# Attention block: the output projection as three products of rounded parts, with the parts made on GpSimd

## The chip, the cores and the metric

The kernel is one program on one core of a Trainium2 chip. The metric is the device time of one execution in microseconds (us). A core has five engines with queues of their own: TensorE (PE, matrix products; PEld is its loading of weights), VectorE (DVE), ScalarE (ACT), GpSimd (POOL) and SyncE (SP), which here issues the transfers. They meet only at semaphores: an instruction adds to one when it is done, and another engine's queue waits until it has reached a number.

## The reference, cut to what matters

The program computes, on an input of 8 x 512 x 256: a delta-rule attention, a feed-forward block, the attention block of this case, and the same feed-forward block again, each with a layer norm before and the input added behind. The attention block has 16 query heads in 4 groups, each group with one key and one value head of 128:

```python
x = x + attn_b(layernorm(x), Wq, Wk, Wv, Wg, Wd, Wo)

# inside attn_b; b = 8, s = 512, 4 groups n of 4 heads g, head size 128
scores = einsum('bngqd,bnkd->bngqk', q, k) * scale
logits = where(causal & (bias > 0), scores + bias, neg)
p = softmax(logits, axis=-1)
o = einsum('bngqk,bnkd->bngqd', p, v)
o = o.transpose(0, 3, 1, 2, 4).reshape(b, s, 16 * 128)
return o @ Wo                      # Wo: 2048 x 256
```

Everything is float32. The change is in the last line.

## The kernel before

The program is a row of five stages, each with its own buffers and semaphores: tables, delta rule, first feed-forward (names `f_`), attention (names `a_`), second feed-forward (names `h_`). Between two stages all engines meet.

In the attention stage the work is cut into 32 turns. Turn t is batch b and group n (t = 4b + n); `here` and `there` are the buffers of even and odd turns. All turns but those of the first and last batch lie in a hardware loop that covers two batches. Each engine's order within a turn is written out by hand in its `turn` function, and everything that an engine waits for is a semaphore count. A turn handles four heads g, shifted against each other so that the engines overlap. For head g:

- TensorE computes the query (`query`, three products of rounded parts), then the scores of four row tiles (`scores`), tiles 0 and 1 before the next query and tiles 2 and 3 behind it. Two PSUM banks `sc` take turns, so tile i + 2 needs tile i read.
- VectorE reads each score tile in `logits` (L2146: score tile in PSUM and bias in SBUF to `pr`, and a row minimum `low`); ScalarE takes the exponentials; VectorE scales the rows in `normalise` (three small chained instructions, L2172 to L2174, and four scalings, L2176, of 128 to 512 columns).
- TensorE transposes the probabilities (`turn_probs`) and multiplies them with the values (`values`, into the one bank `out`); VectorE adds the tail rows and stores the result (`head_out`, L2166) to `oT`, 128 channels x 512 rows, in a slot for each head. `values` of the next head waits for that.

The output projection of turn t - 1 stands in turn t, in two halves of two row tiles each (`project_out`, L1828): the first behind `values` of head 0, the second behind `values` of head 1. A half is 8 full-precision products of 128x128 by 128x256, summed over the four heads; the trace records two matmuls for each. Its end is counted in `y`. VectorE adds a half to the residual `x` (`add_out`, L2186). In the turn, behind the second `add_out`, VectorE makes the low part of the next-but-one turn's query and key weights (`split_w`, L2120). In turns with n = 2 and 3 TensorE computes value rows of the next batch behind the second half; in turn n = 2 it also computes the gate rows.

A "rounded part" is float32r, a shortened float32 that TensorE takes in fewer passes: x_hi is x written as float32r, x_lo is x - x_hi written as float32r, and `product` sums hi x hi, lo x hi and hi x lo.

GpSimd has little to do in this stage: in each turn a diagonal matrix of flags (`diagonals`, L2306) and three copies of bias rows (`spread`, L2298). The projection's weights come by a transfer for each turn (`load_wo`) into two buffers `wo`, and `oT` has two buffers as well, so a projection of turn t - 1 and the heads of turn t don't meet.

Of the kernel before, what the change touches and what calls it, by code (L numbers as in the profile page):

```python
# [10 lines left out]
ALU = mybir.AluOpType  # L11
# [4 lines left out]
P = 128  # L16
# [1567 lines left out]
def attention(nc, io, sems, src, dst):  # L1584
# [6 lines left out]
    with ExitStack() as ctx:  # L1591
# [8 lines left out]

        s = {n: sems[f"a_{n}"] for n in ATTN_SEMS}
        const = sb("const", [P, NCONST])
        cc = {k: const[:, lo:hi] for k, (lo, hi) in CONSTS.items()}
        ident = cc["ident"]
# [10 lines left out]
        wv_hi, wv_lo = (sb(f"wv_{i}", [P, KD, NK * P], F32R) for i in ("hi", "lo"))  # L1615
        wo = two("wo", [P, G, D])
        xl, x, xn = sb("xl", [P, TT, D]), two("x", [P, TT, D]), sb("xn", [P, TT, D])
# [14 lines left out]
        pt = two("pt", [P, L * TT - P * 6])  # L1632
        oT = two("oT", [P, G, L])

# [25 lines left out]
        def _(sp):  # L1660
# [10 lines left out]

            def load_wo(n, tp_):
                sp.dma_start(wo[tp_][:], io["wo_b"][n * G * P:(n + 1) * G * P].rearrange("(g p) d -> p g d", p=P)).then_inc(s[f"wo{tp_}"], 16)

# [11 lines left out]
            load_norm(0)  # L1686
            sp.dma_start(const[:], io["consts"]).then_inc(s["in"], 16)
            load_w(0)
# [15 lines left out]
            def turn(b, bp, n, t, begin, more):  # L1704
                if more or n < 2:
                    sp.wait_ge(s["w_lo"], t + 2)
                    load_w((n + 2) % HKV)
                if not (isinstance(t, int) and t < 2):
                    sp.wait_ge(s["y"], 2 * t - 2)
                load_wo(n, n % 2)  # L1710
                head = isinstance(b, int) and b == 0
                if n == 0 and more:
                    sp.wait_ge(s["xn"], b + 1)
                    load_norm(b + 1)
                if n == 1:
                    if not head:
                        store(b - 1, 1 - bp)
                if n == 2 and more:
                    if not head:
                        sp.wait_ge(s[f"out{1 - bp}"], 8 * b + 8 * bp)  # L1720
                        load_x(b + 1, 1 - bp)
                    sp.wait_ge(s["keep"], b + 2)
                    if not head:
                        sp.wait_ge(s["bp"], HKV * b)
                        sp.wait_ge(s["bd"], HKV * b)
                    else:
                        sp.wait_ge(s["wv_lo"], 1)
                    spread(b + 1, 1 - bp)
# [8 lines left out]
        def _(pe):  # L1737
# [85 lines left out]
            def project_out(t, tp_, half):  # L1823
                if half == 0:
                    pe.wait_ge(s["oT"], G * t + G)
                for j, m in enumerate((2 * half, 2 * half + 1)):
                    for g in range(G):
                        mm = M.matmul(pb[:, j * D:(j + 1) * D], oT[tp_][:, g, m * P:(m + 1) * P], wo[tp_][:, g, :], start=(g == 0), stop=(g == G - 1))  # L1828
                mm.then_inc(s["y"], 1)

            def wo_count(t, n):

                return 8 * t + (0 if n % 2 == 0 else 8)

            def turn(b, bp, n, t, begin, more):
# [52 lines left out]
                if not begin:  # L1888
                    pe.wait_ge(s[f"wo{there}"], wo_count(t, n))
# [69 lines left out]
            values(LAST, HKV - 1, 3, 1)  # L1959
            pe.wait_ge(s["wo1"], 8 * B * HKV)  # L1960
            pe.wait_ge(s["xadd"], 2 * LAST)
# [106 lines left out]
        def _(dve):  # L2068
# [93 lines left out]
            def head_out(t, tp_, g):  # L2162

                dve.wait_ge(s["pv"], G * t + g + 1)
                dve.wait_ge(s["frow"], t + 1)
                V.tensor_tensor(oT[tp_][:, g, :], out[:], tl[tp_][:], ALU.add).then_inc(s["oT"], 1)  # L2166

# [117 lines left out]
        def _(pool):  # L2285
# [15 lines left out]
            def diagonals(t):  # L2301

                pool.wait_ge(s["fl"], t + 1)
                if not (isinstance(t, int) and t == 0):
                    pool.wait_ge(s["ftr"], t)
                Gp.tensor_tensor(dg[:], cc["ident"].unsqueeze(1).to_broadcast([P, TAIL, P]), fl[:].unsqueeze(2).to_broadcast([P, TAIL, P]),  # L2306
                                 ALU.mult).then_inc(s["dg"], 1)

            def turn(b, bp, n, t, begin, more):
# [12 lines left out]
            loop(pool, turn)  # L2322


ATTN_SEMS = ["xl", "x0", "x1", "in", "w", "wv", "wo0", "wo1", "out0", "out1", "kept", "kb0", "kb1",
             "gd", "gd_hi", "gd_lo", "tr", "x_hi", "x_lo", "gt", "gc", "sig", "keep", "vp", "v", "vtp", "vtT", "dg", "one", "w_hi", "w_lo", "wv_hi", "wv_lo",
# [81 lines left out]
```

## Time and profile before

| | before |
| --- | --- |
| median of 3 runs | 4455.96 us (4451.16 to 4456.58) |
| profiled execution, its own time | 4464.27 us |
| its span, first to last instruction | 4462.2 us |
| TensorE busy over the span | 4129.1 us (93%) |
| VectorE | 3010.4 us (67%) |
| ScalarE | 2183.5 us (49%) |
| GpSimd | 1201.0 us (27%) |
| mean granted TensorE clock | 0.973 |

The attention stage lies between about 2898 us and 4241 us of the span. A row of the timeline gives start, duration, engine, line of the kernel, operation, output <- inputs, shape and count; in brackets stands how long the engine was idle before it and which instruction ended that. A row of the groups gives the total, the mean in ns, and the idle time before. Matmuls overlap: the distance of two starts tells what one costs, not its duration. The two levels of TensorE's clock are 2.4 GHz (granted clock 1.0) and 1.2 GHz (0.5).

### The profile page before, as it was taken

The numbers are of one execution on the slowest core, as the hardware profiler recorded it, in microseconds if no ns is written. First come the engines' busy times: TensorE is split into PE (matmuls) and PEld (weight loads), VectorE is DVE, ScalarE is ACT, GpSimd is POOL, SyncE is SP. The second block draws the span as 40 slices with busy tenths as digits, with TensorE's granted clock in tenths as the row PEclk, the third lists the DMA queues.
The fourth block names the chain that finished last, engine by engine and source line by source line (L and its number), as shares of the span: only waits on it lengthen the run. The fifth ranks groups of instructions, "written<-read, shape, count | busy, mean of one in ns | idle before, by whom it ended". The sixth has DMA issues, their size and how long they took to land. (4 is left out here: it accounts for less than half of the span.)

```text
span 4462.2 us, 97071 instructions
## 1 busy us (share of the span) xinstructions
PE 4129.1 (93%) x32143; PEld 3442.7 (77%) x32143; DVE 3010.4 (67%) x7897; ACT 2183.5 (49%) x5660; POOL 1201.0 (27%) x2727
## 2 busy tenths in 40 slices
PE   3499999999999999999999779879999999999979
PEld 3388888888888888888888668767777777778768
DVE  5577777777777777777777345346776776776655
ACT  2255555555555555555555234334444444444344
POOL 5244444444444444444444100000000000000000
PEclk9999999999999999999999689979999999999989
DMA  6433433333333343333333132131111111111021
GB/s 253 150 100 101 120 114 106 106 102 109 100 110 99 107 123 106 104 110 100 109 100 101 59 134 85 41 98 41 38 51 52 52 32 52 52 47 42 15 68 34
DMA packets 558447, 393.06 MB, mean 88 GB/s; under 512 B 253040, under 2 KB 504944, under 8 KB 556400
## 3 DMA queue, kind: packets, MB, share of 16 engines
q1 hardware_dynamic: 557936, 386.69, 28.1%
q8 instruction: 267, 4.37, 0.4%
q14 instruction: 244, 2.00, 0.2%
HBM read 288.36 MB, written 98.14 MB: 87 GB/s over the span
## 5 line engine op out<-in xcount | busy, mean ns | idle before, releaser
L962 DVE SCALAR_TENSOR_TENSOR g_conv<-g_r,g_taps,g_conv 128x511 f32<-128x511 f32 (+2 forms) x961 | 700.0, 742 | 135.9 <-ACT g_conv L847 127.6
L851 ACT ACTIVATE g_us<-g_chn 128x128 f32<-128x128 f32 x528 | 146.6, 278 | 688.4 <-PE g_chn L646 687.6
L2001 ACT ACTIVATE a_pr<-a_pr,a_low 128x128 f32<-128x128 f32 (+3 forms) x512 | 286.6, 560 | 396.2 <-DVE a_low L2146 380.3
L1152 POOL TENSOR_TENSOR g_prod<-g_small 64x14 f32<-64x14 f32 (+6 forms) x896 | 227.0, 253 | 665.8 <-DMA g_small<-lower_d 600.2
L571 PE MATMUL g_r<-g_x_hi,g_w_hi 128*128 128x512 f32 x770 | 366.9, 477 | 9.6 <-issue 7.1
L2146 DVE CUSTOM_DVE_ANT_0 a_pr<-a_sc,a_bias 128x128 f32<-128x128 f32 (+3 forms) x512 | 242.2, 486 | 193.2 <-issue 174.2
L2306 POOL TENSOR_TENSOR a_dg<-a_const,a_fl 128x384 fp32r<-128x384 f32 x32 | 26.4, 826 | 1154.5 <-DVE a_fl L2153 1154.5
L571 PE MATMUL g_r<-g_x_hi,g_w_lo 128*128 128x512 f32 x770 | 306.8, 398 | 0.0
L571 PE MATMUL g_r<-g_x_lo,g_w_hi 128*128 128x512 f32 x770 | 305.0, 396 | 0.0
L1820 PE MATMUL a_out<-a_pt,a_v 128*128 128x512 f32 (+3 forms) x1024 | 297.9, 434 | 0.9 <-DVE a_oT L2166 0.9
L847 ACT ACTIVATE g_conv<-g_r,g_taps 128x512 f32<-128x512 f32 x321 | 220.4, 687 | 137.4 <-PE g_r L571 127.0
L1820 PEld LDWEIGHTS a_out<-a_pt,a_v 128*128 128x128 f32 x1024 | 185.0, 191 | 103.1 <-issue 62.6
L995 DVE SCALAR_TENSOR_TENSOR g_R<-g_chn,g_ctab,g_bv 128x128 f32<-128x128 f32 x462 | 160.4, 347 | 150.9 <-PE g_chn L638 136.7
L1154 POOL TENSOR_TENSOR g_small<-g_small,g_prod 64x14 f32<-64x14 f32 (+6 forms) x896 | 240.6, 269 | 70.3
L1828 PE MATMUL a_pb<-a_wo,a_oT 128*128 128x256 f32 x1024 | 231.8, 379 | 1.7 <-DVE a_oT L2166 0.9
L1003 DVE SCALAR_TENSOR_TENSOR g_S<-g_S,g_ctab,g_chn 128x128 f32<-128x128 f32 x396 | 137.2, 346 | 134.7 <-PE g_chn L656 134.7
L646 PE MATMUL g_chn<-g_R,g_U 128*128 128x128 f32 x924 | 213.9, 314 | 8.3 <-DVE g_R L995 6.9
L638 PE MATMUL g_chn<-g_S,g_kT 128*128 128x128 f32 x924 | 205.1, 304 | 13.8 <-DVE g_S L1001 10.9
L658 PE MATMUL g_ob<-g_us,g_at 128*128 128x128 f32 x1056 | 214.6, 286 | 0.4 <-ACT g_us L851 0.4
L987 DVE TENSOR_TENSOR g_U<-g_U,g_lev 64x128 f32<-64x128 f32 x520 | 147.8, 284 | 93.7 <-PE g_lev L611 88.2
L1828 PEld LDWEIGHTS a_pb<-a_wo,a_oT 128*128 128x128 f32 x1024 | 189.7, 190 | 25.3 <-DVE a_x L2186 1.2
L1745 PE MATMUL a_sc<-a_k_hi,a_q_hi 128*128 128x128 f32 (+3 forms) x512 | 185.4, 362 | 25.6 <-DVE a_low L2146 19.0
(355 smaller groups left out, 11714.6 us busy)
## 6 DMA issues: line engine op xcount, KB each, us to landing
g_w_hi<-ws_d SPq DMA_DIRECT2D x65, 768.0 KB, 5.5
g_w_lo<-ws_d SPq DMA_DIRECT2D x65, 768.0 KB, 6.7
lower_d<-g_L SPq DMA_DIRECT2D x64, 512.0 KB, 3.3
g_T<-low_d SPq DMA_DIRECT2D x64, 512.0 KB, 4.1
g_U<-upp_d SPq DMA_DIRECT2D x64, 512.0 KB, 5.4
a_w<-w_groups SPq DMA_DIRECT2D x32, 640.0 KB, 4.5
oT_d<-g_oT SPq DMA_DIRECT2D x67, 256.0 KB, 5.4
f_oT<-oT_d SPq DMA_DIRECT2D x8, 2048.0 KB, 9.4
```

The source lines that it names most:

```text
L571: mm = M.matmul(BANK[n][:], a[:, k, n, :], c[:, k, :], start=(i == 0), stop=(i == len(terms) - 1))
L638: M.matmul(chn[:, 0, :], keys[:, c, :], S[c % 2][:], start=True, stop=True).then_inc(s["d_ks"], 1)
L646: M.matmul(chn[:, 1, :], U[par][:, c, :], bv[par][:, 0, :] if c == 0 else R[:], start=True, stop=True).then_inc(s["d_u"], 1)
L658: mm = M.matmul(dst, at[(q + 2) % QN][:, c, :], us[:], start=(c % 2 == 0), stop=False)
L847: A(conv[TURN[n] % 2][:], BANK[n][:], ACT.Copy, scale=taps[par][:, n, CONV - 1:CONV]).then_inc(s["d_tap"], 1)
L962: ins = V.scalar_tensor_tensor(out=y[:, k:L], in0=x[:, 0:L - k], scalar=tap, in1=y[:, k:L], op0=ALU.mult, op1=ALU.add)
L1152: ch.link(G.tensor_tensor(prod[:, 0:SM - 1 - k, 0:k], small[:, k + 1:SM, k:k + 1].to_broadcast(shape), small[:, k:k + 1, 0:k].to_broadcast ...
L1154: ch.link(G.tensor_tensor(rest, rest, prod[:, 0:SM - 1 - k, 0:k], ALU.subtract))
L1820: mm = M.matmul(out[:, k * P:L], v[bp][:, k, at], pt[g % 2][:, first[k]:first[k] + L - k * P], start=(k == 0), stop=(k == TT - 1))
L1828: mm = M.matmul(pb[:, j * D:(j + 1) * D], oT[tp_][:, g, m * P:(m + 1) * P], wo[tp_][:, g, :], start=(g == 0), stop=(g == G - 1))
L2001: A(pr[g % 2][:, i, 0:width(i)], pr[g % 2][:, i, 0:width(i)], ACT.Exp, scale=-1.0, bias=low[g % 2][:, i:i + 1], accum_out=tot[g % 2][:, i: ...
L2146: V.tensor_tensor_reduce(pr[g % 2][:, i, 0:width(i)], sc[i % 2][:, 0:width(i)], bias[tp_][:, i, 0:width(i)], -SCALE, 3.0e38, ALU.add, ALU. ...
```

## The change

The projection becomes a `product` of rounded parts: three products in place of one full-precision product, 24 matmuls in a half. GpSimd makes the parts: `split_head` those of a head's output (a multiplication with ones that writes float32r, then a subtraction, 128x512 each), `split_wo` those of the turn's weights (128x1024 each). `oT` is now two buffers of one head each; the parts `o_hi`, `o_lo`, `wo_hi`, `wo_lo` and the loaded weights `wo` exist once. So `split_wo(t)` and the heads 0 to 2 of turn t wait for `y` at 2t, the end of the projection of turn t - 1; `head_out` waits until its buffer's former head has been split; `project_out` waits for the parts, and the load of the weights for the split of those before. GpSimd's order in a turn is: diagonals, head 3 of the turn before, bias rows, weights, heads 0, 1 and 2. The stage loads only the 1808 columns of the constants that it uses, out of 2320.

```diff
-        const = sb("const", [P, NCONST])
+        USED = CONSTS["pick_group"][1]
+        const = sb("const", [P, USED])
-        wo = two("wo", [P, G, D])
+        wo = sb("wo", [P, G, D])
+        wo_hi, wo_lo = (sb(f"wo_{i}", [P, G, D], F32R) for i in ("hi", "lo"))
-        oT = two("oT", [P, G, L])
+        oT = two("oT", [P, L])
+        o_hi, o_lo = (sb(f"o_{i}", [P, G, L], F32R) for i in ("hi", "lo"))
...
-                if not (isinstance(t, int) and t < 2):
-                    sp.wait_ge(s["y"], 2 * t - 2)
-                load_wo(n, n % 2)
+                if not begin:
+                    sp.wait_ge(s["wo_lo"], t)
+                load_wo(n)
...
             def project_out(t, tp_, half):
                 if half == 0:
-                    pe.wait_ge(s["oT"], G * t + G)
+                    pe.wait_ge(s["o_lo"], G * t + G)
+                    pe.wait_ge(s["wo_lo"], t + 1)
                 for j, m in enumerate((2 * half, 2 * half + 1)):
-                    for g in range(G):
-                        mm = M.matmul(pb[:, j * D:(j + 1) * D], oT[tp_][:, g, m * P:(m + 1) * P], wo[tp_][:, g, :], start=(g == 0), stop=(g == G - 1))
+                    at = slice(m * P, (m + 1) * P)
+                    mm = product(pb[:, j * D:(j + 1) * D], [(o_hi[:, g, at], o_lo[:, g, at], wo_hi[:, g, :], wo_lo[:, g, :]) for g in range(G)])
                 mm.then_inc(s["y"], 1)
...
                 dve.wait_ge(s["frow"], t + 1)
-                V.tensor_tensor(oT[tp_][:, g, :], out[:], tl[tp_][:], ALU.add).then_inc(s["oT"], 1)
+                if not (isinstance(t, int) and G * t + g < 2):
+                    dve.wait_ge(s["o_lo"], G * t + g - 1)
+                V.tensor_tensor(oT[g % 2][:], out[:], tl[tp_][:], ALU.add).then_inc(s["oT"], 1)
...
+            def split_head(t, g):
+                pool.wait_ge(s["oT"], G * t + g + 1)
+                Gp.tensor_tensor(blocks(o_hi[:, g, :]), blocks(oT[g % 2][:]), by_one(TT), ALU.mult).then_inc(s["o_hi"], 1)
+                pool.wait_ge(s["o_hi"], G * t + g + 1)
+                Gp.tensor_tensor(o_lo[:, g, :], oT[g % 2][:], o_hi[:, g, :], ALU.subtract).then_inc(s["o_lo"], 1)
+
+            def split_wo(t):
+                flat = lambda m: m[:].rearrange("p g d -> p (g d)")
+                pool.wait_ge(s["wo"], 16 * t + 16)
+                Gp.tensor_tensor(blocks(flat(wo_hi)), blocks(flat(wo)), by_one(G * D // P), ALU.mult).then_inc(s["wo_hi"], 1)
+                pool.wait_ge(s["wo_hi"], t + 1)
+                Gp.tensor_tensor(flat(wo_lo), flat(wo), flat(wo_hi), ALU.subtract).then_inc(s["wo_lo"], 1)
+
             def turn(b, bp, n, t, begin, more):
...
                 diagonals(t)
+                if not begin:
+                    split_head(t - 1, G - 1)
                 if nxt:
...
                     spread(1 - n % 2, (n + 1) % HKV, nb, 8 * b - 8 * bp + 16 if n < HKV - 1 else 8 * b + 8 * bp + 16)
+                if not begin:
+                    pool.wait_ge(s["y"], 2 * t)
+                split_wo(t)
+                for g in range(G - 1):
+                    split_head(t, g)
...
             loop(pool, turn)
+            split_head(LAST, G - 1)
```

## Rows read from the trace of the kernel before

**Rows 1.** Stretch: length, busy (x instructions) of PE, PEld, DVE, ACT, POOL; clock; DMA.
```profile
3100.00:4240.00 1140.00, 1105.56 (x5764) 895.16 (x5762) 795.93 (x2842) 525.17 (x1365) 69.31 (x109) 0.99 0.14 43
```

**Rows 2.** Timeline of TensorE, a turn with n = 1.
```profile
3515.14 3.62 PE L1828 MATMUL a_pb<-a_wo,a_oT 128*128 128x256 f32 x16
...
3518.66 0.28 PE L1745 MATMUL a_sc<-a_k_hi,a_q_lo 128*128 128x128 f32 x1
...
3518.88 0.33 PE L1745 MATMUL a_sc<-a_k_hi,a_q_hi 128*128 128x256 f32 x1
3519.05 0.28 PE L1745 MATMUL a_sc<-a_k_hi,a_q_lo 128*128 128x256 f32 x1
...
3521.16 0.44 PE L1745 MATMUL a_sc<-a_k_hi,a_q_hi 128*128 128x384 f32 x1 [0.31 <-DVE a_low L2146]
...
3528.75 0.45 PE L1745 MATMUL a_sc<-a_k_hi,a_q_hi 128*128 128x384 f32 x1 [0.32 <-DVE a_low L2146]
```

**Rows 3.** Timeline of TensorE in the first feed-forward stage, first and last of 46.
```profile
2886.07 0.28 PE L1318 MATMUL f_wide<-f_w_lo,f_h_hi 128*128 128x256 f32 x1
...
2891.17 0.28 PE L1318 MATMUL f_wide<-f_w_lo,f_h_hi 128*128 128x256 f32 x1
```

**Rows 4.** GpSimd's groups; the last row: ns least/median/most, first and last start.
```profile
L1165 POOL TENSOR_TENSOR g_dmt<-g_dmt,g_const 128x512 f32<-128x512 f32 x64 | 82.2, 1284 | 3.2 <-ACT g_dmt L866 2.2 <-issue 1.0
...
L1568 POOL TENSOR_TENSOR f_xb<-f_x,f_b 128x1024 f32<-128x1024 f32 x8 | 19.2, 2400 | 265.6 <-DVE f_mark L1482 265.6
...
L2306 POOL TENSOR_TENSOR a_dg<-a_const,a_fl x32: 825/826/828, 2968.2 to 4197.3; 128x384 fp32r<-128x384 f32 x32
```

**Rows 5.** Timeline of VectorE in the turn of rows 2.
```profile
3518.80 0.69 DVE L2186 TENSOR_TENSOR a_x<-a_x,a_pb 128x512 f32<-128x512 f32 x1 [2.42 <-PE a_pb L1828]
3519.40 1.48 DVE L2120 TENSOR_TENSOR a_w_lo<-a_w,a_w_hi 128x1280 fp32r<-128x1280 f32 x1
...
3524.91 0.53 DVE L2173 TENSOR_TENSOR a_cnt<-a_cnt,a_tot 128x4 f32<-128x4 f32 x1
...
3525.69 1.59 DVE L2176 TENSOR_SCALAR a_pr<-a_pr,a_rec 128x128 f32<-128x128 f32 x4
3527.20 0.68 DVE L2166 TENSOR_TENSOR a_oT<-a_out,a_tl 128x512 f32<-128x512 f32 x1
...
3576.99 0.16 DVE L2173 TENSOR_TENSOR a_cnt<-a_cnt,a_tot 128x4 f32<-128x4 f32 x1
...
3577.40 1.27 DVE L2176 TENSOR_SCALAR a_pr<-a_pr,a_rec 128x128 f32<-128x128 f32 x4
```

**Rows 6.** Timeline of GpSimd in that turn: the bias rows.
```profile
3524.45 1.75 POOL L2298 TENSOR_TENSOR a_bias<-a_kb,a_start 128x128 f32<-128x128 f32 x3
```

**Rows 7.** Timeline of the first stage: the first of four GpSimd splits, VectorE's scalings.
```profile
12.89 3.42 POOL L230 TENSOR_TENSOR t_wh_hi<-t_wh,t_const 128x1536 fp32r<-128x1536 f32 x1 [9.65 <-DMA t_wh<-w_heads]
...
13.90 12.96 DVE L320 TENSOR_SCALAR t_xn<-t_x,t_mv,t_rstd 128x256 f32<-128x256 f32 x4
```

**Rows 8.** Timeline of VectorE and TensorE, a turn with n = 2 and the start of the next.
```profile
3561.28 0.69 DVE L2186 TENSOR_TENSOR a_x<-a_x,a_pb 128x512 f32<-128x512 f32 x1 [2.41 <-PE a_pb L1828]
...
3565.61 0.33 PE L1745 MATMUL a_sc<-a_k_hi,a_q_hi 128*128 128x384 f32 x1
...
3573.56 0.33 PE L1745 MATMUL a_sc<-a_k_hi,a_q_hi 128*128 128x384 f32 x1
```

**Rows 9.** Timeline of TensorE, a turn with n = 0: the query behind the key.
```profile
3623.17 0.50 PE L1745 MATMUL a_pa<-a_x_hi,a_w_hi 128*128 128x512 f32 x1 [0.73 <-DVE a_k_lo L2134]
```

**Rows 10.** Timeline of TensorE at the end of the stage: the last projections.
```profile
4221.81 3.62 PE L1828 MATMUL a_pb<-a_wo,a_oT 128*128 128x256 f32 x16
...
4232.83 3.69 PE L1828 MATMUL a_pb<-a_wo,a_oT 128*128 128x256 f32 x16 [0.88 <-DVE a_oT L2166]
```

**Rows 11.** Timeline of TensorE, one long idle; granted clock (third last number) behind it.
```profile
3447.13 0.32 PE L1745 MATMUL a_sc<-a_k_hi,a_q_hi 128*128 128x128 f32 x1 [3.21 <-issue]
...
3448.00:3463.00 15.00, 14.66 (x71) 11.74 (x70) 7.77 (x31) 4.95 (x14) 0.00 (x0) 0.77 0.01 2
```

More of the change, by code:

```diff
@@ L1601, in attention @@
         s = {n: sems[f"a_{n}"] for n in ATTN_SEMS}
-        const = sb("const", [P, NCONST])
-        cc = {k: const[:, lo:hi] for k, (lo, hi) in CONSTS.items()}
+        USED = CONSTS["pick_group"][1]
+        const = sb("const", [P, USED])
+        cc = {k: const[:, lo:hi] for k, (lo, hi) in CONSTS.items() if hi <= USED}
         ident = cc["ident"]
@@ L1670, in load_w, with load_wo @@
                 sp.dma_start(w[:], io["w_groups"][n, :, :, 0:GW]).then_inc(s["w"], 16)
-            def load_wo(n, tp_):
-                sp.dma_start(wo[tp_][:], io["wo_b"][n * G * P:(n + 1) * G * P].rearrange("(g p) d -> p g d", p=P)).then_inc(s[f"wo{tp_}"], 16)
+            def load_wo(n):
+                sp.dma_start(wo[:], io["wo_b"][n * G * P:(n + 1) * G * P].rearrange("(g p) d -> p g d", p=P)).then_inc(s["wo"], 16)
             def spread(b, bp):
@@ L1686, in _ @@
             load_norm(0)
-            sp.dma_start(const[:], io["consts"]).then_inc(s["in"], 16)
+            sp.dma_start(const[:], io["consts"][:, 0:USED]).then_inc(s["in"], 16)
             load_w(0)
@@ L1824, in project_out @@
                 if half == 0:
-                    pe.wait_ge(s["oT"], G * t + G)
+                    pe.wait_ge(s["o_lo"], G * t + G)
+                    pe.wait_ge(s["wo_lo"], t + 1)
                 for j, m in enumerate((2 * half, 2 * half + 1)):
-                    for g in range(G):
-                        mm = M.matmul(pb[:, j * D:(j + 1) * D], oT[tp_][:, g, m * P:(m + 1) * P], wo[tp_][:, g, :], start=(g == 0), stop=(g == G - 1))
+                    at = slice(m * P, (m + 1) * P)
+                    mm = product(pb[:, j * D:(j + 1) * D], [(o_hi[:, g, at], o_lo[:, g, at], wo_hi[:, g, :], wo_lo[:, g, :]) for g in range(G)])
                 mm.then_inc(s["y"], 1)
-            def wo_count(t, n):
-                return 8 * t + (0 if n % 2 == 0 else 8)
             def turn(b, bp, n, t, begin, more):
@@ L1888, in turn @@
                 if not begin:
-                    pe.wait_ge(s[f"wo{there}"], wo_count(t, n))
                     if n == 0 or not more:
@@ L1959, in _ @@
             values(LAST, HKV - 1, 3, 1)
-            pe.wait_ge(s["wo1"], 8 * B * HKV)
             pe.wait_ge(s["xadd"], 2 * LAST)
@@ L2307, in diagonals @@
                                  ALU.mult).then_inc(s["dg"], 1)
+            by_one = lambda n: cc["ones"].unsqueeze(1).to_broadcast([P, n, P])
+            blocks = lambda ap: ap.rearrange("p (n c) -> p n c", c=P)
+            def split_head(t, g):
[9 more added lines that the diff above has]
+                Gp.tensor_tensor(flat(wo_lo), flat(wo), flat(wo_hi), ALU.subtract).then_inc(s["wo_lo"], 1)
             def turn(b, bp, n, t, begin, more):
@@ L2322, in _ @@
             loop(pool, turn)
-ATTN_SEMS = ["xl", "x0", "x1", "in", "w", "wv", "wo0", "wo1", "out0", "out1", "kept", "kb0", "kb1",
+            split_head(LAST, G - 1)
+ATTN_SEMS = ["xl", "x0", "x1", "in", "w", "wv", "wo", "wo_hi", "wo_lo", "o_hi", "o_lo", "out0", "out1", "kept", "kb0", "kb1",
              "gd", "gd_hi", "gd_lo", "tr", "x_hi", "x_lo", "gt", "gc", "sig", "keep", "vp", "v", "vtp", "vtT", "dg", "one", "w_hi", "w_lo", "wv_hi", "wv_lo",
```

## The prediction

> **What bounds the kernel now.** I read the page first, then the stretches of the attention stage, then one turn on TensorE, VectorE and GpSimd side by side. The change lies in the attention stage alone. It runs from about 2898 us to 4241 us. In its steady part TensorE is busy 97% of the time at a granted clock of 0.99, VectorE 70% and GpSimd 6% [rows 1]. So TensorE sets the time, and GpSimd looks like a free engine. What the shares hide is how tightly VectorE follows TensorE. In the turn around 3515 us TensorE already idles twice, 0.31 and 0.32 us, each time before the third score tile of a head, until `logits` has read the bank (L2146) [rows 2]. Whatever delays VectorE ahead of those two places is lost by TensorE one for one.
>
> **The products.** A half of the projection is 16 recorded matmuls (two for each of 8 full-precision products). The first starts at 3515.14; the next work's second matmul starts at 3518.66, and such matmuls are 0.11 apart (3518.66 to 3518.88 holds two intervals) [rows 2], so the half takes 3.52 - 0.11 = 3.4 us. The new half is 24 matmuls on rounded parts, 256 columns wide. The feed-forward stage has just that stream: from 2886.07 to 2891.17 us there are 45 starts of this shape, 0.113 us apart [rows 3]. 24 x 0.113 = 2.7 us. Saved: 0.68 us per half, 64 halves, 43.5 us. The lower bound comes from the score product of 256 columns behind one of 128, whose first interval is 0.17 (18.88 to 19.05) [rows 2]; if each of the 8 groups paid it, a half would take 8 x 0.40 = 3.2 us and the saving would be 13 us. I take 43.5, the row of the same shape.
>
> **What GpSimd gets.** The tensor operations in its list with two streamed operands give the price: 1.28 us for 128x512, 2.40 us for 128x1024 [rows 4]. A head is two of 128x512 (2.54 us), the weights are two of 128x1024 (4.7 us): 4 x 2.54 + 4.7 = 14.9 us in a turn of 39.6 us (31 turns between the first and the last start of the diagonals, L2306) [rows 4], beside 0.83 + 1.75 = 2.6 us now [rows 4, 6]. The capacity is there. The place is the trouble. The weights of a turn are split only after y(2t), the end of the second projection half, because `wo_hi` and `o_hi` are single; head 0 is split behind them. So right after each second half GpSimd works 4.7 + 2.5 + 2.5 us without a pause, head 1 included.
>
> **The wait of head_out.** VectorE's `head_out(t,2)` now waits for head 0's parts, 7.3 us after y. Before, it starts 8.4 us after the add that follows y (3518.80 to 3527.20) [rows 5]. By itself this wait is just hidden.
>
> **VectorE beside GpSimd.** This is the large term. At 3524.91 a 128x4 addition of two SBUF operands (L2173) takes 0.53 us where its other calls take 0.16, and the four scalings after it take 1.59 us where 1.27 is usual [rows 5]; in exactly that time GpSimd is copying bias rows [rows 6]. The first stage shows it large: four scalings of 128x256 take 12.96 us while GpSimd runs its 3.42 us splits one behind the other [rows 7]. That is one VectorE instruction per GpSimd instruction. VectorE's work on PSUM with one SBUF operand (L2146, L2166) keeps its length. The Trainium skill, page "SBUF — State Buffer", section "SBUF: two separate sides", calls this an exclusive lock on a port pair shared by the two engines, taken by a DVE instruction in a 2-port mode or with two SBUF inputs, and held for the whole instruction. It speaks against this change, and the trace agrees; with full GpSimd durations as the blocks its rule would make the loss of a turn some 0.5 us larger than what I take next.
>
> I walk through a turn with the times after the add of half two (zero at 3518.80, [rows 5]).
> - Turns with n = 0 or 1 (no value rows behind the half). GpSimd's first weight split covers 0.05 to 2.4. `split_w` (L2120, two SBUF operands, 1.48 us) wants 0.60 and gets in at about 2.2: `logits` is 1.6 late, and TensorE, which already waits there, loses 1.6. Then the second weight split and head 0 hold GpSimd until 7.5 to 8.7, head 1 until 10.2 to 11.4. In this time fall the count instruction (L2172), the addition (L2173) and the four scalings of `normalise`. They are chained, so each of the three gets in behind another GpSimd instruction, the four scalings together behind one: end at 11.3 to 12.5 instead of 8.5. `head_out` and the next `logits` are 2.8 to 4.0 late in all, and TensorE with them. I take 3.5 us. There are 15 such turns: 52 us (42 to 62).
> - Turns with n = 2 or 3 (value rows first). Zero is 3561.28 [rows 8]. `split_w` is late by 1.6 again and ends at 3.7; `logits` behind it has read the first tile at 4.1. TensorE, with the value rows before it, wants the third tile at 3565.61, which is 4.33 [rows 8]: nothing lost. `normalise` then ends 1.5 to 2.1 late. The next `logits` stands behind it, with 1.1 us of slack before TensorE wants its third score tile at 3573.56 [rows 8]; 0.4 to 1.0 is lost. I take 0.8, 14 turns: 11 us (0 to 18).
> - The diagonal of the mask (L2126, two SBUF operands) meets the split of head 3, up to 0.85 us. Behind it VectorE makes the key's low part, for which TensorE already waits 0.73 us in a turn with n = 0 [rows 9]; there and in the others the wait for ScalarE's part or the gate and value rows cover most of it. 0.15 us x 30: 5 us (0 to 15).
>
> **The end of the stage.** The last turn has no further scores behind half two, which starts at 4221.81 and ends 3.4 us later, at 4225.2. Before, the last projection starts at 4232.83 [rows 10]. Now it comes after 4.7 + 4 x 2.54 us of GpSimd work, with its hops 15.6 us after 4225.2, at 4240.8: +8 us. Nothing hides this. The bound below is 7, above 11 with the slow clock.
>
> **The clock.** After TensorE's idle of 3.21 us at 3447.13 the granted clock falls to a mean of 0.77 over the next 15 us, that is 7 us of the stretch at the lower level (1.2 instead of 2.4 GHz) [rows 11]. The new idle comes in two pieces, each under 2 us. I add 5 us (0 to 40).
>
> **Small ones.** The constants shrink from 2320 to 1808 columns, once, ahead of the stage's first matmul; no row prices it, a gain under 1 us, left out of the sum. The weights' load waits for the split of the turn before (about 6 us after y) and has 25 us left. On GpSimd `diagonals` moves behind head 2 and `spread` behind head 3. Head 2 can only be split once `head_out(t,2)` has run, so behind a turn with n = 1 the diagonals are ready at about 16.6 us after the zero, while TensorE does the scores, the transposes and the values of head 3 that stand ahead of their matmul (L1797): hidden, but by little. This cover is the next to go: with GpSimd later still, TensorE waits for the diagonals. `spread` is needed only at the end of the turn. Extra semaphore clears: nothing, under 0.5 us.
>
> **Sum.** 52 + 11 + 5 + 8 + 5 - 43.5 = +37.5 us. The profiled execution took 4464.27 us, its span 4462.2, the median of the three runs 4455.96; I carry the same difference over: 4456 + 37.5 = 4493 us. The likeliest case has a range of its own of 4460 to 4530: the low bounds give 42 + 7 - 44 = +5, the high ones, with 10 us of clock and a saving of 35, 62 + 18 + 15 + 11 + 10 - 35 = +81, which takes all blocks at once.
>
> **Rivals.**
> 1. The products decide and the blocks are mostly absorbed. For it: VectorE is idle 30% of the stage. Against: [rows 5, 7]. Then -43.5 + 7 = -37, 4419 us; with a fifth of the 68 us of blocks left, 4432. It decides in favour as soon as the blocked turns cost under 1.2 us on the mean. Chance 0.16.
> 2. The blocks are worse. GpSimd could get in between the four unchained scalings of `normalise` as well, as it did between the chained ones of [rows 7]; another two blocks of 1.0 us in 29 turns is +58, and with the clock falling in the 15 turns with two idle pieces (3.4 us each, [rows 11]) +50. That gives 4550 to 4600. Chance 0.14.
> 3. Gain and loss cancel within 9 us: the low bounds of my own case. Chance 0.08.
> 4. My case: 0.62.
>
> 0.2% (9 us) is about what a measurement of this kernel can tell from no change. Faster: rival 1, 0.16. Same: 0.08. Slower: 0.76. The range for 8 in 10 goes from 4432 to 4560.
>
> **What the changed profile would show.** The projection's 24 matmuls per half should start 0.113 us apart. TensorE's share in the steady part should fall from 97% to about 90%, with its idle put down to `a_low` L2146 and to what follows `split_w`. `split_w` should last about 3 us instead of 1.48, L2173 and L2176 should have means well over 0.25 and 0.40 us. GpSimd's new instructions should last 1.27 and 2.35 us. Before the last projection TensorE should idle about 8 us more. I am wrong if `split_w` keeps 1.48 us beside a running GpSimd split (then rival 1), if the three-part products start more than 0.13 us apart, or if GpSimd's instructions are themselves stretched by VectorE, so that the wait for `o_lo` in `head_out` becomes the one that ends last.

## The result and the profile after

The changed kernel (called after from here on, as the old one is called before) takes 4529.18 us (median of 4 runs, 4523.01 to 4533.61) against 4456.27 us (4451.16 to 4459.46): ratio 1.0156, 95% interval 1.0143 to 1.0169, 72.9 us slower. The forecast was 4493, in a range of 4432 to 4560: the direction was right, the loss twice as large as forecast (37.5). The profiled execution took 4533.61 us. First the page of after, span and busy shares:

```profile
span 4531.8 us, 98557 instructions
...
PE 4120.6 (91%) x32655; PEld 3455.3 (76%) x32655; DVE 3140.7 (69%) x7897; ACT 2180.1 (48%) x5660; POOL 1722.9 (38%) x3047
```

The stretches of after (columns as in [rows 1]): the steady part, which answers to [rows 1], and the whole attention stage.

```profile
3100.00:4300.00 1200.00, 1098.97 (x6248) 905.46 (x6246) 920.37 (x2867) 526.72 (x1379) 545.20 (x404) 0.96 0.14 41
...
2931.00:4313.00 1382.00, 1249.05 (x7014) 1029.77 (x7013) 1035.04 (x3222) 596.01 (x1550) 601.58 (x448) 0.95 0.14 41
```

The same whole stage before:

```profile
2935.00:4242.00 1307.00, 1255.51 (x6497) 1015.62 (x6497) 902.89 (x3222) 599.71 (x1550) 81.72 (x128) 0.98 0.14 44
```

All of the loss is here: 75 us, with 4 us less ahead of the stage. TensorE's share in the steady part is 92%. Over the whole stage its idle rises from 51.5 to 133 us, and its busy time, which the cheaper products should have cut by over 40 us, falls by 6 at a lower granted clock (0.95 instead of 0.98). That looks like two losses of their own, 80 us of waits and 40 us of clock. The last two experiments show that much of the second is hidden in the first.

GpSimd's and VectorE's groups of after:

```profile
L2317 POOL TENSOR_TENSOR a_o_lo<-a_oT,a_o_hi 128x512 fp32r<-128x512 f32 x128 | 171.6, 1341 | 10.0
...
L2325 POOL TENSOR_TENSOR a_wo_lo<-a_wo,a_wo_hi 128x1024 fp32r<-128x1024 f32 x32 | 109.3, 3414 | 2.5
...
L2118 DVE TENSOR_TENSOR a_w_lo<-a_w,a_w_hi 128x1280 fp32r<-128x1280 f32 x30 | 95.4, 3179 | 0.0
...
L2173 DVE TENSOR_TENSOR a_cnt<-a_cnt,a_tot 128x4 f32<-128x4 f32 x128 | 50.2, 392 | 4.4
...
L2151 DVE TENSOR_SCALAR a_fl<-a_low 128x3 f32<-128x3 f32 x32 | 26.9, 839 | 1.1
```

`split_w` (L2118 now) takes 3.18 us instead of 1.48 on average over these 30 calls; 29 of them take 3.16 us or more. Who waits for whom on TensorE (us in total, times, longest), in after from 2980 to 4300 us:

```profile
PE a_sc L1748 <- DVE a_low L2144: 80.6, 46, 5.0
PE a_pa L1748 <- DVE a_k_lo L2132: 10.0, 13, 1.4
PE a_out L1823 <- DVE a_oT L2166: 5.1, 1, 5.1
```

and before, from 2980 to 4230 us:

```profile
PE a_sc L1745 <- DVE a_low L2146: 13.6, 38, 3.0
```

Up to the last turn TensorE does not wait for a part made by GpSimd. It waits for `logits` on VectorE, 67 us more than before. One turn with n = 0 (the half's add, L2186, to the first `logits` of the next head) on VectorE, after:

```profile
3167.02 0.69 DVE L2186 TENSOR_TENSOR a_x<-a_x,a_pb 128x512 f32<-128x512 f32 x1 [0.20 <-PE a_pb L1748]
3167.62 3.25 DVE L2118 TENSOR_TENSOR a_w_lo<-a_w,a_w_hi 128x1280 fp32r<-128x1280 f32 x1
...
3173.74 0.62 DVE L2151 TENSOR_SCALAR a_fl<-a_low 128x3 f32<-128x3 f32 x1
...
3175.74 1.19 DVE L2173 TENSOR_TENSOR a_cnt<-a_cnt,a_tot 128x4 f32<-128x4 f32 x1
...
3177.18 2.16 DVE L2176 TENSOR_SCALAR a_pr<-a_pr,a_rec 128x128 f32<-128x128 f32 x4
...
3179.87 0.28 DVE L2144 CUSTOM_DVE_ANT_0 a_pr<-a_sc,a_bias 128x128 f32<-128x128 f32 x1
```

and on GpSimd in the same time:

```profile
3167.15 2.38 POOL L2323 TENSOR_TENSOR a_wo_hi<-a_wo,a_const 128x1024 fp32r<-128x1024 f32 x1 [18.05 <-PE a_pb L1748]
3169.61 3.50 POOL L2325 TENSOR_TENSOR a_wo_lo<-a_wo,a_wo_hi 128x1024 fp32r<-128x1024 f32 x1
3173.07 1.26 POOL L2315 TENSOR_TENSOR a_o_hi<-a_oT,a_const 128x512 fp32r<-128x512 f32 x1
...
3175.64 1.28 POOL L2315 TENSOR_TENSOR a_o_hi<-a_oT,a_const 128x512 fp32r<-128x512 f32 x1
3176.99 1.28 POOL L2317 TENSOR_TENSOR a_o_lo<-a_oT,a_o_hi 128x512 fp32r<-128x512 f32 x1
```

`split_w` ends 1.34 us after GpSimd's first weight split (3169.53), so it did nearly all of its 1.48 us of work behind it. The addition L2173 ends at 3176.93, where the split begun at 3175.64 ends (3176.92). From the add to the next `logits` VectorE needs 12.85 us. TensorE pays at two places, each ahead of the third score tile of a head (first and second place from here on); here the turn with n = 0 and the next:

```profile
3171.15 0.44 PE L1748 MATMUL a_sc<-a_k_hi,a_q_hi 128*128 128x384 f32 x1 [2.08 <-DVE a_low L2144]
3180.21 0.44 PE L1748 MATMUL a_sc<-a_k_hi,a_q_hi 128*128 128x384 f32 x1 [0.60 <-DVE a_low L2144]
...
3210.93 0.44 PE L1748 MATMUL a_sc<-a_k_hi,a_q_hi 128*128 128x384 f32 x1 [2.08 <-DVE a_low L2144]
3220.63 0.45 PE L1748 MATMUL a_sc<-a_k_hi,a_q_hi 128*128 128x384 f32 x1 [2.44 <-DVE a_low L2144]
```

The end of the stage on TensorE: last matmul of half two, then the start of the last projection. Between them lie the two idles that GpSimd's parts do cause: 5.1 us before the values of head 3, since the `head_out` of head 2 waits 6.2 us for `a_o_lo`, and 3.51 us before the projection, until GpSimd's last subtraction ends at 4302.85.

```profile
4286.93 0.28 PE L1748 MATMUL a_pb<-a_wo_lo,a_o_hi 128*128 128x256 f32 x1
...
4302.95 0.55 PE L1748 MATMUL a_pb<-a_wo_hi,a_o_hi 128*128 128x256 f32 x1 [3.51 <-issue]
```

### The profile page after: what moved, and what is told of

It is laid out like the page before. It is cut to its first block and busy times, and to the rows that moved or that the text cites. A ratio compares the mean times of both kernels' runs of the same rounds, so it can differ in the third digit from the quotient of the medians.

```text
span 4531.8 us, 98557 instructions
## 1 busy us (share of the span) xinstructions
PE 4120.6 (91%) x32655; PEld 3455.3 (76%) x32655; DVE 3140.7 (69%) x7897; ACT 2180.1 (48%) x5660; POOL 1722.9 (38%) x3047
## 5 line engine op out<-in xcount | busy, mean ns | idle before, releaser
L2323 POOL TENSOR_TENSOR a_wo_hi<-a_wo,a_const 128x1024 fp32r<-128x1024 f32 x32 | 76.2, 2382 | 541.6 <-PE a_pb L1748 541.6
L1143 POOL TENSOR_TENSOR g_gsum<-g_tab,g_const 128x512 fp32r<-128x512 f32 x65 | 68.0, 1047 | 513.5 <-DMA g_tab<-tab_d 513.4
L2315 POOL TENSOR_TENSOR a_o_hi<-a_oT,a_const 128x512 fp32r<-128x512 f32 x128 | 163.5, 1277 | 185.4 <-DVE a_oT L2166 185.4
```

## The experiments

The times of different runs are compared as they stand. The kernel before was measured again beside them, and its median was 4456 to 4462 us, so a difference of two such times is good to some 6 us.

**What does GpSimd's work cost?** The parts are made of 4 columns only; the rest of each is filled with ones once. The other three operations are cut in the same way. Nearly all of the projection's values are left out. All waits and all of TensorE's work stay.

```diff
-                Gp.tensor_tensor(blocks(o_hi[:, g, :]), blocks(oT[g % 2][:]), by_one(TT), ALU.mult).then_inc(s["o_hi"], 1)
+                Gp.tensor_tensor(o_hi[:, g, 0:4], oT[g % 2][:, 0:4], cc["ones"][:, 0:4], ALU.mult).then_inc(s["o_hi"], 1)
...
```

> The changed kernel with all its waits, buffers and orders, but GpSimd makes the parts of 4 columns only (both splits of a head and both of the weights), each about 0.2 us; the rest of the parts is filled once with ones, so most of the projection's values are left out. If the loss comes from VectorE being held behind GpSimd's long instructions, it is gone and the gain of the products is left: 4456 - 43 = 4413 us, 4405 to 4425, and split_w lasts 1.48 us. If it comes from the new waits (single buffers, the weights only after y), most of it stays: above 4480.

Measured: 4417.18 us, ratio 0.9899 (0.9881 to 0.9917). `split_w` is at 1.49 us again, L2173 at 0.175. So the waits and the order cost nothing that shows; the length of GpSimd's instructions costs 112 us (4529.2 - 4417.2), with what the clock does in consequence. The same turn on VectorE in this kernel:

```profile
3153.41 0.69 DVE L2186 TENSOR_TENSOR a_x<-a_x,a_pb 128x512 f32<-128x512 f32 x1 [0.20 <-PE a_pb L1748]
3154.01 1.49 DVE L2118 TENSOR_TENSOR a_w_lo<-a_w,a_w_hi 128x1280 fp32r<-128x1280 f32 x1
...
3159.53 0.16 DVE L2173 TENSOR_TENSOR a_cnt<-a_cnt,a_tot 128x4 f32<-128x4 f32 x1
...
3159.94 1.28 DVE L2176 TENSOR_SCALAR a_pr<-a_pr,a_rec 128x128 f32<-128x128 f32 x4
...
3161.73 0.29 DVE L2144 CUSTOM_DVE_ANT_0 a_pr<-a_sc,a_bias 128x128 f32<-128x128 f32 x1
```

8.32 us to the next `logits`, against 12.85.

**What do the products give?** All of GpSimd's work stays, and the projection is done as before, in full precision, on the high parts; the low parts are made and not used.

```diff
-                    mm = product(pb[:, j * D:(j + 1) * D], [(o_hi[:, g, at], o_lo[:, g, at], wo_hi[:, g, :], wo_lo[:, g, :]) for g in range(G)])
+                    for g in range(G):
+                        mm = M.matmul(pb[:, j * D:(j + 1) * D], o_hi[:, g, at].bitcast(F32), wo_hi[:, g, :].bitcast(F32), start=(g == 0), stop=(g == G - 1))
```

> The changed kernel with GpSimd's work and all waits, but the projection is again one full-precision product, of the high parts alone (the low parts are made and not used). If TensorE's saving of 0.68 us per half comes through in full in the changed kernel, this takes 43 us more than it: 4572 us. If TensorE gives part of it back by waiting for VectorE, less: 4540 to 4560. Were the saving an error of mine, 4529.

Measured: 4577.61 us, ratio 1.0254 (1.0237 to 1.0271). The products give back 48.4 us (4577.6 - 4529.2); the prediction had 43.5. Beside this run the kernel before took 5.6 us more than beside the change, and by the two ratios (1.0254 and 1.0156) it is 44 us. In the traces a turn with n = 2 at full clock is 1.45 us longer than in after, 46 us in 32 turns. So the saving lies between 44 and 48 us.

**Is it what GpSimd reads, or that it runs?** Each split becomes a 4-column operation and a fill of a buffer that nobody reads (no input, 0.95 us each, one for each part of a head, two for each part of the weights). The values are left out as in the first run.

```diff
+                Gp.tensor_tensor(o_hi[:, g, 0:4], oT[g % 2][:, 0:4], cc["ones"][:, 0:4], ALU.mult)
+                Gp.memset(fill[:, 0, :], 1.0).then_inc(s["o_hi"], 1)
...
```

> The changed kernel with GpSimd's splits replaced by one operation on 4 columns and fills of a scratch buffer, meant to last about as long as the splits (a fill reads nothing from SBUF); parts filled once with ones, so the projection's values are left out. If only GpSimd's reads hold VectorE up: like small parts plus the late end, 4413 + 8 = 4421 us. If any long GpSimd instruction does: about 4520. If it holds up the one-operand scalings and the flags but not the instructions with two SBUF operands, between: 4450 to 4490, with split_w at 1.48 us and L2176 and L2151 long.

Measured: 4442.92 us, ratio 0.9951 (0.9935 to 0.9968). The groups on VectorE, lines shifted by one:

```profile
L2119 DVE TENSOR_TENSOR a_w_lo<-a_w,a_w_hi 128x1280 fp32r<-128x1280 f32 x30 | 44.5, 1484 | 0.0
...
L2152 DVE TENSOR_SCALAR a_fl<-a_low 128x3 f32<-128x3 f32 x32 | 25.9, 811 | 1.1
...
L2174 DVE TENSOR_TENSOR a_cnt<-a_cnt,a_tot 128x4 f32<-128x4 f32 x128 | 22.4, 175 | 4.4
...
3165.61 2.63 DVE L2177 TENSOR_SCALAR a_pr<-a_pr,a_rec 128x128 f32<-128x128 f32 x4
```

Beside a GpSimd that only writes, VectorE's instructions with two SBUF operands run free (1.48 and 0.175 us), while the short one with a single SBUF operand is still at 0.81 instead of 0.17 (0.73 without its first call, which stands beside the one-time filling of the parts). The four scalings, also of one SBUF operand, take 2.63 us instead of 1.27 in the turns with n = 0 and 1 (the last row is one of them). The Trainium skill, page "SBUF — State Buffer", section "Who interferes with whom", states this division: a VectorE instruction with two SBUF inputs is blocked only by a GpSimd instruction that reads SBUF, one in a 2-port mode by any. The trace agrees for the instructions with two SBUF inputs; in which mode the others run, it does not show. GpSimd is busy 108 us less here than in after (1614.7 against 1722.9), so the 86 us between the two runs (4529.2 - 4442.9) are not all due to the reads.

**Would another order help?** GpSimd's split of the weights waits for VectorE's `split_w`.

```diff
                 if not begin:
                     pool.wait_ge(s["y"], 2 * t)
+                    if more or n < 2:
+                        pool.wait_ge(s["w_lo"], t + 3)
                 split_wo(t)
```

> The changed kernel, complete, with one wait more: GpSimd starts the weights' split only when VectorE's split_w of the turn is done. split_w goes from a mean of 3.18 us back to 1.48, which by my walk gives back 1.6 us in each of the 15 turns with n = 0 or 1; GpSimd is 1.4 us later, so flags and normalise meet more of it. By the theory of the blocks a gain of 0 to 25 us: 4505 to 4529. If late parts (the wait of head_out) were what matters: 20 to 40 us slower.

Measured: 4576.45 us, ratio 1.025 (1.0233 to 1.0267): a clear miss, 47 us slower than after instead of somewhat faster. `split_w` is free indeed (1484 ns), but GpSimd's 10 us of work now begin 2 us later and lie over all of `normalise`. VectorE in a turn with n = 2, the addition and the four scalings:

```profile
3616.79 1.29 DVE L2173 TENSOR_TENSOR a_cnt<-a_cnt,a_tot 128x4 f32<-128x4 f32 x1
...
3618.33 3.09 DVE L2176 TENSOR_SCALAR a_pr<-a_pr,a_rec 128x128 f32<-128x128 f32 x4
```

The scalings take 3.09 us instead of 1.27: a GpSimd instruction gets in between them, though they aren't chained (4.26 us in turns with n = 0 and 1). That is the mechanism of rival 2; in after the four take 2.0 to 2.2 us in all turns but the last two. Yet `head_out`, which stands behind them, starts only 0.5 to 0.7 us later than in after, some 17 us in 30 turns. The rest of the 47 goes with the clock: behind the halves of the turns with n = 1 TensorE's two idle places are of 0.3 and 4.7 us instead of 2.08 and mostly 2.4, and the granted clock up to the next second half is 0.89 instead of mostly 0.96. No run separates the two parts. My picture, that the block of `split_w` can be saved by itself, fell: a block avoided comes back at the next VectorE instruction of the kind, as long as GpSimd's list is as long.

**Weights or heads?** Weights split in full, heads of 4 columns (the heads' values are left out):

```diff
...
-                Gp.tensor_tensor(o_lo[:, g, :], oT[g % 2][:], o_hi[:, g, :], ALU.subtract).then_inc(s["o_lo"], 1)
+                Gp.tensor_tensor(o_lo[:, g, 0:4], oT[g % 2][:, 0:4], o_hi[:, g, 0:4], ALU.subtract).then_inc(s["o_lo"], 1)
...
```

> The changed kernel with the weights' parts in full and the heads' parts of 4 columns only (filled once with ones; most of the projection's values are left out). The mirror of weights from DRAM. By the theory split_w stays at 2.4 us or more, normalise (5.9 us after the add) is nearly free: small parts plus 1.6 us in the n = 0 and 1 turns plus the flags, 4417 + 26 + 5 = 4448 us. If the two costs simply added, this loss and that of the run with weights from DRAM would make 4529 - 4417 = 112 us; I expect less than that from the two, since back to back they reach into normalise.

Measured: 4468.24 us, ratio 1.0015 (1.0001 to 1.003), 20 above what was expected. Its ten runs spread from 4457 to 4481. The weights alone cost 51 us over the first run, and `split_w` is at 3.18, `normalise` free. A turn with n = 0 in this kernel, and then the same turn with small parts:

```profile
3159.74:3198.06 38.32, 36.14 (x206) 29.63 (x204) 28.51 (x96) 17.74 (x47) 10.45 (x14) 0.96 0.14 46
...
3153.41:3188.26 34.85, 34.43 (x206) 28.33 (x204) 26.66 (x96) 17.45 (x47) 6.06 (x14) 1.00 0.17 50
```

The turn is 3.5 us longer. TensorE starts the third score tile at the first place 4.13 us after the add instead of 2.37, so 1.8 us are the block on `split_w`, which is what was expected. The other 1.7 come behind that place, where TensorE waits for nothing at the second place and the granted clock from 3165 to 3170 is at a mean of 0.66. Over the 14 stretches from n = 0 and 1 ahead of the last batch the block makes 25 us and the slow stretches 24. The expectation had 26 and nothing: what it missed is the clock.

**The weights' parts once, from DRAM.** GpSimd splits the weights in the first batch only. SyncE stores the parts and loads them back; from the second batch on it loads them in each turn behind y(2t). Nothing is left out.

```diff
-                    pe.wait_ge(s["wo_lo"], t + 1)
+                    pe.wait_ge(s["wop"], 32 * t + 32)
...
+                if head:
...
+                        sp.dma_start(io["wos_d"][n, i], m[:].rearrange("p g d -> p (g d)").bitcast(F32)).then_inc(s["wos"], 16)
+                    sp.wait_ge(s["wos"], 32 * (t + 1))
+                else:
+                    sp.wait_ge(s["y"], 2 * t)
+                for i, m in enumerate(parts):
+                    sp.dma_start(m[:].rearrange("p g d -> p (g d)").bitcast(F32), io["wos_d"][n, i]).then_inc(s["wop"], 16)
```

> The changed kernel, complete, but GpSimd splits each group's weights only in the first batch; SyncE stores the parts to DRAM and loads them from there for every turn. Heads as in the change. By the theory of the blocks split_w loses its long wait (mean under 2.0 us) and normalise meets less of GpSimd, since head 0 and head 1 are done 5.2 us after y instead of 11: 4435 to 4465 us. If the loss sat in the heads' splits alone, it stays above 4500.

Measured: 4452.82 us, ratio 0.9981 (0.9971 to 0.999). The heads alone cost 36 us over the first run; 36 + 51 = 87 is less than the 112 of both, as expected: with both, GpSimd's list reaches into `normalise`. But some 20 of the 51 are clock, which in after is mostly hidden behind waits, so this isn't a sum of blocks alone.

**The same, and ScalarE makes the heads' high parts.** Four subtractions a turn are left to GpSimd.

```diff
+            def head_hi(t, g):
+                act.wait_ge(s["oT"], G * t + g + 1)
+                A(o_hi[:, g, :], oT[g % 2][:], ACT.Copy).then_inc(s["o_hi"], 1)
...
```

> As weights from DRAM, and ScalarE makes a head's high part (a copy that writes float32r, 0.6 us), so GpSimd has only the four subtractions of a turn, 1.3 us each. By the theory the loss against small parts shrinks with GpSimd's time: 4420 to 4435 us, faster than before the change. If ScalarE's copies delay its exponentials: above 4450.

Measured: 4420.17 us (4412.97 to 4423.15), ratio 0.9909 (0.9893 to 0.9926), with the whole computation done: faster than both kernels. TensorE's waits for `a_low` are back where they were (13.3 us), `split_w` is at 1.65. A step further, with VectorE making the low part too, between the second and third score tile of `logits` (0.72 us each, GpSimd has none of it):

```diff
+                for i in range(TT):
+                    if i == 2:
+                        for args in gap:
+                            head_lo(*args)
...
```

> As the run before, and VectorE makes a head's low part, placed between the second and third score tile of logits, where it idles 0.5 to 1.5 us; GpSimd makes no part but the first batch's weights. If VectorE's gaps hold the four subtractions of 0.69 us: 4410 to 4425 us, the whole gain of the products. If VectorE was not free there, each costs up to 0.69 us: 64 to 88 us more, 4480 to 4500.

Measured: 4428.18 us, ratio 0.9926 (0.9909 to 0.9942), 8 us behind the run before and just above the expectation: VectorE's own 90 us of subtractions cost somewhat more than the four blocks a turn that are left on GpSimd.

**How much of the loss is the clock?** By TensorE's busy time 40 us of the loss are lower clock. To test it, all of the change is kept and work is added: 8 matmuls of 512 columns, 1.86 us, that nobody uses, in the first place behind the halves of turns with n = 0 and 1.

```diff
                     query(t + 1, there, nb, 1)
+                    if n < 2 and not begin:
+                        pe.wait_ge(s["xadd"], 2 * t)
+                        for i in range(8):
+                            M.matmul(pb[:], wv_hi[:, 0, 0:P], wv_hi[:, 0, :], start=(i == 0), stop=(i == 7))
                     scores(t + 1, 0, there, (2, 3))
```

> The changed kernel, all of its work kept, with work added that nobody uses: 8 rounded matmuls of 512 columns (0.232 us apart in the value rows, 1.86 us) into the free bank pb, put into TensorE's idle place of 2.08 us ahead of the third score tile behind the second projection half, in the 15 turns with n = 0 or 1. Theory A, the clock: this idle place makes the granted clock fall in the stretches behind it, and some 40 us of the change's cost are lost so. Then TensorE's clock falls less often, and although work was only added, the time falls by 10 to 35 us, to 4495 to 4520, with TensorE's waits for a_low falling by about 15 x 1.9 = 28 us in the list of waits. Rival B, the place of the work: the half clock comes from elsewhere, or the blocks on VectorE set the end of each turn whatever TensorE's clock is. Then the time stays at 4529 or rises by up to 5 us.

Measured: 4536.87 us, ratio 1.0179 (1.0165 to 1.0193), 8 us slower than after. Neither reading had it right: the first place is closed (0.25 us), but the second is now at 2.27 us behind the halves of turns with n = 0, where it was 0.6 in most. The stretch at half clock moves with it. In after it lies between the places,

```profile
3172.00:3177.00 5.00, 5.00 (x19) 3.74 (x18) 4.42 (x12) 3.02 (x9) 4.84 (x5) 0.66 0.80 218
```

and with one filler behind the second, which ends at 3170.25:

```profile
3170.50:3175.50 5.00, 5.00 (x19) 3.81 (x19) 4.18 (x17) 3.59 (x11) 2.90 (x3) 0.66 0.00 0
```

So the second place was filled too:

```diff
                 query(t, here, bp, 2)
+                if n in (1, 2) and not begin:
+                    pe.wait_ge(s["ptv"], G * t)
+                    pe.wait_ge(s["pta"], 2 * G * t)
+                    for i in range(8):
+                        M.matmul(tp[0][:], wv_hi[:, 0, 0:P], wv_hi[:, 0, :], start=(i == 0), stop=(i == 7))
                 scores(t, 1, here, (2, 3))
```

> The run with one filler, and the same 8 rounded matmuls (1.86 us, results unused, all real work kept) also in the second idle place, ahead of the third score tile of head 1 in turns with n = 1 and 2, that is behind the halves of the 15 turns with n = 0 and 1. There the run with one filler idles 2.27 to 2.45 us each time. Reading A: behind the add of half two VectorE works without a gap up to the second place (3039.39 to 3052.8 in the changed kernel), so it sets when TensorE goes on; the time lost to the clock is what lies behind the second place. Then with both places filled the granted clock stays up behind both, the idle put down to a_low falls by about 25 us more (65.8 to about 40), and the time falls from 4537 by 10 to 30 us, to 4507 to 4527. Rival B: the clock's fall costs nothing of its own, because VectorE and GpSimd set the pace of the whole turn. Then the time stays at 4537 or rises by up to 10 us through the added matmuls.

Measured: 4525.39 us, ratio 1.0149 (1.0132 to 1.0166). TensorE's idle for `a_low` is 40.0 us as expected, and the time falls by 11.5 us against one filler, though work was added; against after it is 4 us less, within the spread. The clock stays up in all seven stretches from a turn with n = 0, but only in two of the first seven from n = 1. What matters is in the turns. The stretch from the second add of a turn with n = 0 to that of the next turn, then the same with n = 1, in this kernel at clock 1.00:

```profile
3163.68:3203.52 39.84, 38.43 (x222) 31.26 (x220) 31.88 (x97) 17.46 (x47) 18.88 (x14) 1.00 0.15 44
3537.81:3579.57 41.76, 40.85 (x243) 33.68 (x241) 33.27 (x104) 17.87 (x48) 18.87 (x14) 1.00 0.21 60
```

in after, n = 0 and n = 1:

```profile
3167.02:3206.80 39.78, 36.40 (x206) 29.57 (x204) 31.49 (x97) 17.63 (x47) 18.83 (x14) 0.96 0.15 44
...
3206.80:3250.11 43.31, 38.73 (x227) 31.91 (x225) 33.24 (x104) 17.89 (x48) 18.86 (x14) 0.96 0.20 57
```

before:

```profile
3158.02:3194.76 36.74, 36.13 (x190) 28.86 (x188) 27.35 (x97) 17.46 (x47) 2.54 (x4) 1.00 0.15 47
3355.43:3394.72 39.29, 38.60 (x211) 31.13 (x209) 28.62 (x103) 17.89 (x48) 2.54 (x4) 1.00 0.23 67
```

and with one filler, n = 0:

```profile
3157.01:3198.17 41.16, 38.04 (x214) 31.04 (x212) 31.96 (x96) 17.48 (x47) 18.87 (x14) 0.96 0.14 42
```

The turn with n = 0 is 39.84 us long at full clock and 39.78 us with a stretch at half clock in it: that stretch lies between the two places, where TensorE would wait for VectorE anyway, and costs nothing. Behind the second place it costs 1.3 to 1.6 us (41.16 against 39.84; 43.31 against 41.76, where it lies at 3230).

## Why the prediction was right, and by what it was too small

The shortest turns, from the starts of the second adds, give what a turn loses; the products' 48.4/32 = 1.5 us are added back. All are at full clock but the one of after with n = 0, which is as long as that of two fillers at full clock; for n = 1 that of two fillers stands. The column of the prediction leaves out its 0.15 us for the diagonal.

| turn | before | after | lost | predicted |
| --- | --- | --- | --- | --- |
| n = 0 | 36.7 | 39.8 | 4.6 | 3.5 |
| n = 1 | 39.3 | 41.8 | 4.0 | 3.5 |
| n = 2 | 40.2 | 39.9 | 1.2 | 0.8 |
| n = 3 | 41.3 | 41.8 | 2.0 | 0.8 |

- **The products.** Right: 0.113 us apart, 44 to 48 us instead of 43.5.
- **VectorE beside GpSimd.** The mechanism was right and carries the sign: `split_w` 3.18 us, L2173 0.39, TensorE's wait on `a_low`. The size was short. For 28 turns (seven of each kind) the unrounded lengths give 81 us against 64 predicted (60, and 4 for the diagonals), and the last three stretches 21 us against 12 (3.5 + 0.8 + 8 for the tail). Of these 9 us 4 are in the last batch's n = 2, which has no value rows and so no cover: 5.1 against 0.8.
- How late VectorE is, the prediction had right in every kind of turn. With n = 0 and 1 `head_out` starts 12.2 to 12.3 us after the add instead of 8.4, 3.8 to 3.9 later (predicted 2.8 to 4.0). With n = 2 and 3 it starts 12.3 us after it instead of 10.26, 2.0 us later, as predicted ("`normalise` then ends 1.5 to 2.1 late"): there the value rows leave VectorE 2.5 us of gaps before the change, and 1.6 of them take up the delay of `split_w`.
- **The step that was short: the slack behind `normalise`.** The prediction read 1.1 us of slack in [rows 8], a turn with n = 2, and used it for n = 3 as well. `head_out` and the third score tile at the second place, before with n = 3:

```profile
3611.80 0.68 DVE L2166 TENSOR_TENSOR a_oT<-a_out,a_tl 128x512 f32<-128x512 f32 x1
3612.75 0.44 PE L1745 MATMUL a_sc<-a_k_hi,a_q_hi 128*128 128x384 f32 x1 [0.18 <-DVE a_low L2146]
```

and in after, the tile with n = 2 (add at 3250.11) and with n = 3 (add at 3290.00):

```profile
3263.38 0.44 PE L1748 MATMUL a_sc<-a_k_hi,a_q_hi 128*128 128x384 f32 x1 [0.83 <-DVE a_low L2144]
...
3303.26 0.44 PE L1748 MATMUL a_sc<-a_k_hi,a_q_hi 128*128 128x384 f32 x1 [2.21 <-DVE a_low L2144]
```

With n = 2 the tile moves from 12.28 us after the add to 13.27: of the 2.0 us one is lost, as the slack of 1.1 says. With n = 3 it moves from 11.22 to 13.26, and all 2.0 are lost. There was no slack: TensorE already waited 0.18 us at this place, because only a turn with n = 2 has more value rows between its values of head 2 and this place (before, they start from 3569.99 to 3571.24). That is 8 of the 17 us.
- The next 6 are with n = 0: the second place is 3.8 us late, and 0.6 us come behind it. There the diagonal (L2124 now) meets the split of head 3 and takes 1.52 us instead of 0.68, and TensorE waits 0.61 us for the key's low part behind it. The prediction had put 0.15 us on every turn for this; it falls on one kind. The rest is the 3.5 of the blocks, taken 0.3 us too low.
- `flags` (L2151) was not costed, and is blocked in nearly every turn (0.84 instead of 0.17 us). That it cost anything of its own isn't shown: in one turn with n = 0 it took 0.17 us, and `head_out` came 12.29 us after the add all the same. In all 28 turns it comes 12.2 to 12.3 us after the add, in the turn shown above 1.0 us after GpSimd's split of head 1 ends (3178.27), whatever was blocked on the way.
- **Waits for the parts.** Right: `head_out` waits for a part once in the stage, in its last turn, 6.2 us, which is part of the tail. Nothing was late for `diagonals` or `spread`.
- **The tail.** Right: 4286.93 to 4302.95 is 16 us, as predicted (15.6), 8 more than before.
- **The clock.** Taken at 5 us. Time above the shortest length of each kind of turn (for after's n = 1 the 41.76 of two fillers) sums to 18 us before and 30 after (28 turns each): 12 us. It isn't the clock's alone; the idle of [rows 11] is in the 18. Of the 40 us that the busy time suggests, the rest is time in which TensorE ran slowly toward a wait that VectorE had set. The two idle places are 2.08 and 0.6 to 2.4 us, not each under 2 us as predicted, and they are not harmless; what they cost depends on which side of the last one the slow stretch lies.
- Together, over the 31 stretches: 81 + 21 + 12 - 31 x 1.5 = 67.5 us, which is by how much the first and the last second add are further apart in after (1272.8 against 1205.4 us). The parts are differences of the same lengths, so that they add up proves nothing. Of the 69.6 us between the two profiled spans another 3.7 lie ahead of the first second add: nearly 8 are lost in the stage's start, 4 gained before it. No run was aimed there.
- **GpSimd's own durations.** 1.28 (1.34 for the subtractions' mean) and 2.38 us as predicted, but the weights' low part takes 3.41: VectorE's `split_w` is between. The blocking goes both ways.
- Rival 1 (blocks absorbed) is refuted by the table; rival 2's extra blocks occur in one turn of after (3.06 us for the four scalings) and in 30 turns with the weights behind `split_w`.
- The forecast was half of what came, and not by errors that cancel: the blocks, the last turns and the clock were all set too low. Only the products' gain, up to 5 us too low, works the other way.

Left open: what the order of GpSimd's list would give with double buffers for the parts, which weren't tried, and what brings the granted clock down in the first place.

## What to carry to other kernels

A free engine is judged by the instructions that run beside its new ones. List VectorE's instructions with operands only in SBUF in that stretch, down to those of three elements, and add a GpSimd duration for each chain link; a delay early in a stretch is still there at its end unless a gap follows, and the slack behind it has to be read in each kind of turn, not in one of them. The transformation was worth having once GpSimd was nearly out of it: constant parts reloaded from DRAM and copies on ScalarE turned +1.6% into -0.9%. And busy time lost to a lower clock need not be time lost: here only what lay behind the last wait counted.

## What the hardware showed unexpectedly

The granted clock falls behind an idle place of 2.08 us, shorter than the 3.21 of [rows 11]: in after such a place ends at 3171.15, and 3172 to 3177 is at a mean of 0.66 (the row stands above). It doesn't do so each time: behind a place of the same 2.08 us in the next turn (3210.93) the first stretch at half clock is at 3230, behind the second place (2.44 us). Nor does it need such a place. Before, TensorE's longest idle places in the 16 us ahead of 3213 are of 0.31 and 0.32 us, and yet the granted clock is at a mean of 0.51 from there:

```profile
3213.00:3217.00 4.00, 4.00 (x17) 3.80 (x18) 0.90 (x7) 1.19 (x5) 0.00 (x0) 0.51 0.00 0
```

What the runs show is that filling both places kept the clock up in the turns with n = 0.

A multiplication of 3 elements a partition on VectorE can take 1.26 us: `flags` in after (ns least/median/most).

```profile
L2151 DVE TENSOR_SCALAR a_fl<-a_low x32: 168/898/1264, 2963.7 to 4255.2; 128x3 f32<-128x3 f32 x32
```
